# Last stage of a graph and expert kernel: more row and result buffers, groups computed ahead placed farther apart, the experts' bias added by TensorE

## What is computed

```python
x = x + segment_sum((layernorm(x) @ W)[src] * weight[:, None], dst) + b
xn = layernorm(x)                       # [12500, 256]
# routing is by the mean over all nodes, so that all nodes share two experts
top_w, top_i = top_k(routing(mean(xn) @ Wr + br), 2);  top_w = softmax(top_w)
y = sum_k top_w[k] * (gelu(xn @ W1[top_i[k]] + b1[top_i[k]]) @ W2[top_i[k]] + b2[top_i[k]])
x = x + layer_norm(y + xn) * gamma + beta
```

## Time and profile before

| | us |
|---|---|
| median of 3 runs | 2519.41 |
| lowest and highest | 2519.26, 2525.82 |
| the profiled execution | 2519.76 |
| its span in the profile | 2518.0 |
| PE busy over the span | 2178.6 |
| DVE, ACT, POOL busy | 1054.8, 1145.3, 1656.8 |
| last stage, first `up` to the last matmul | 2019.4 to 2505.4 |

### The profile page before, as it was taken

How to read it: one execution, slowest core, us unless ns; L and a number is a source line. 1 busy time by engine, 2 the same in 40 slices (tenths; PEclk the granted TensorE clock), 3 DMA queues, 4 the chain that set the end, 5 groups by cost and what they waited for, 6 DMA issues and landing times. The chain is left out here.

```text
span 2518.0 us, 40482 instructions
## 1 busy us (share of the span) xinstructions
PE 2178.6 (87%) x9536; PEld 1651.2 (66%) x9537; DVE 1054.8 (42%) x2962; ACT 1145.3 (45%) x3139; POOL 1656.8 (66%) x1643
## 2 busy tenths in 40 slices
PE   2388898889989988899989989889899889888898
PEld 1266666666767665676666666666676678777787
DVE  7693222232332232232232223223233257778876
ACT  3467666565564444443333233322311265544453
POOL 6577777777777777777777777777777413434332
PEclk9899999999999998999999999999999989999999
DMA  9955555555655555555555546555555422322221
GB/s 339 305 163 163 164 166 162 170 176 173 222 183 177 162 173 158 172 174 172 161 164 168 165 149 193 161 161 166 171 165 172 131 97 93 101 84 84 84 77 54
DMA packets 229382, 401.22 MB, mean 159 GB/s; under 512 B 35813, under 2 KB 150170, under 8 KB 229244
## 3 DMA queue, kind: packets, MB, share of 16 engines
q0 software_dynamic: 75072, 205.10, 27.5%
q1 hardware_dynamic: 153740, 192.37, 23.7%
q10 hardware_dynamic: 432, 2.40, 0.3%
HBM read 323.27 MB, written 76.46 MB: 159 GB/s over the span
## 5 line engine op out<-in xcount | busy, mean ns | idle before, releaser
L515 POOL DMA_INDIRECT G<-xr_d,SRC x1468 | 1390.9, 947 | 447.2 <-issue 297.3
L970 DVE TENSOR_SCALAR OH<-CST,DL,WR 128x128 f32<-128x128 f32 x1564 | 571.0, 371 | 1273.5 <-PE ps L1240 747.0
L1240 PE MATMUL ps<-G,OH 128*128 x3128 | 744.7, 390 | 141.6 <-DVE OH L970 130.1
L1240 PEld LDWEIGHTS ps<-G,OH 128*128 128x128 f32 x3128 | 597.3, 194 | 283.6 <-issue 204.6
L1219 PE MATMUL ps<-YU,W1u 128*128 128x512 f32 x768 | 358.6, 620 | 58.6 <-ACT H L697 31.1
L1230 PE MATMUL ps<-W2u,H 128*128 128x256 f32 x1536 | 347.4, 385 | 7.2 <-issue 6.9
L1230 PEld LDWEIGHTS ps<-W2u,H 128*128 128x128 f32 x1536 | 292.4, 192 | 58.6 <-issue 19.5
L1219 PEld LDWEIGHTS ps<-YU,W1u 128*128 128x128 f32 x768 | 147.7, 198 | 248.5 <-issue 207.3
L704 ACT ACTIVATE YE<-ps 128x512 f32<-128x512 f32 x96 | 57.3, 597 | 445.9 <-PE ps L1230 445.9
L697 ACT ACTIVATE H<-ps,b1a 128x512 f32<-128x512 f32 x192 | 130.9, 687 | 275.6 <-PE ps L1219 275.4
L1072 DVE TENSOR_TENSOR Hlo<-Ht,Hhi 128x512 fp32r<-128x512 f32 (+1 forms) x152 | 135.5, 898 | 115.7 <-ACT Hhi L796 115.6
(11 more groups left out here) (170 smaller groups left out, 2494.5 us busy)
## 6 DMA issues: line engine op xcount, KB each, us to landing
W1u<-in_W SPq DMA_DIRECT2D x48, 512.0 KB
W2u<-in_W SPq DMA_DIRECT2D x48, 512.0 KB
y_d<-YE SPq DMA_DIRECT2D x48, 512.0 KB
G<-xr_d,SRC POOLq DMA_INDIRECT x1468
x_d<-X SPq DMA_DIRECT2D x98, 128.0 KB, 2.5
yt_d<-YT SPq DMA_DIRECT2D x98, 128.0 KB, 2.4
XR<-in_x SPq DMA_DIRECT2D x97, 128.0 KB
XS<-in_x SPq DMA_DIRECT2D x24, 512.0 KB, 12.9
```

Source lines behind the costliest of these rows:

```text
L515: e.indirect_dma_start(out=G[:, s % RING, :], out_offset=None, in_=x if s < FRESH else xr_d, in_offset=bass.IndirectOffsetOnAxis(ap=SRC[:, ...
L970: e.tensor_scalar(OH[:, s % OHR, :], iota, DL[:, s:s + 1], WR[:, s + 1:s + 2], ALU.is_equal, ALU.mult).then_inc(s_oh, 1)
L1240: e.matmul(ps[:, 0, 0:D], OH[:, r, :], Gf[:, bass.ds(g + r * D, D)], start=False, stop=True, skip_group_check=True).then_inc(s_main, 1)
```

## The change

- `XL` gets a fourth buffer, and SP loads item n + 4 behind item n. `Z` and its statistics get a third buffer. `XN` keeps three. SP loads four `XL` at the start of the stage.
- The groups computed ahead stand behind `post[1]`, `[3]`, `[6]`, `[9]`, `[11]` and `[14]`.
- Of the 19 post groups POOL no longer adds the bias (L523 stays for the six groups computed ahead). DVE splits the bias once into a high and a low row, `B2r`, in four small instructions. In `down(k, 7)` each tile gets one more matmul, 2 partitions by 128x256, that adds both rows: 74 in all.
- POOL adds the rows of two items ahead before `rstd`, if the next item is a group computed ahead.
- `YP[0]` takes the room of `W2s`, so the first four `YP` loads wait until the low half of W2 is made. The load of `YL` for `post[2]` now goes ahead of them.
- In the first part some semaphores are merged (x, xr, router loads). Who waits for what stays.

```diff
-            if k >= 1 and k % 2 == 1 and len(pre_of) < AHEAD:
-                pre_of[k] = len(pre_of)
-                order.append(pre_of[k])
+        pre_of = {1 + (len(post) - 3) * a // AHEAD: a for a in range(AHEAD)}
+        order = [n for k, g in enumerate(post) for n in ((g, pre_of[k]) if k in pre_of else (g,))]
...
-            for n in range(3):
+            for n in range(4):
                 load_x1(n)
...
-            e.wait_ge(s_w1l, 2)
-            for a in range(2):
-                load_y(a)
...
             load_yl(2)
+            e.wait_ge(s_w1l, 2)
+            e.wait_ge(s_w2l, 2)
+            for a in range(2):
+                load_y(a)
...
-                if n + 3 < NG:
-                    load_x1(n + 3)
+                if n + 4 < NG:
+                    load_x1(n + 4)
...
-                e.wait_ge(s_b2, 2)
-                e.tensor_tensor(out=XN[:, n % 3, 0:m, :], in0=XN[:, n % 3, 0:m, :], in1=B2[:, :].unsqueeze(1).to_broadcast([P, m, D]), op=ALU.add).then_inc(s_xb, 1)
+                if g < AHEAD:
+                    e.wait_ge(s_b2, 2)
+                    e.tensor_tensor(out=XN[:, n % 3, 0:m, :], in0=XN[:, n % 3, 0:m, :], in1=B2[:, :].unsqueeze(1).to_broadcast([P, m, D]), op=ALU.add).then_inc(s_xb, 1)
...
-            add_rows(0)
+            added = 0
             for n in range(NG):
-                if n + 1 < NG:
-                    add_rows(n + 1)
+                until = min(n + (2 if n + 1 < NG and order[n + 1] < AHEAD else 1), NG - 1)
+                while added <= until:
+                    add_rows(added)
+                    added += 1
                 rstd(n)
...
+            e.wait_ge(s_b2, 2)
+            e.tensor_copy(B2h[:, :], B2[0:2, :]).then_inc(s_b2, 1)
+            e.wait_ge(s_b2, 3)
+            e.tensor_tensor(out=B2l[:, :], in0=B2[0:2, :], in1=B2h[:, :].bitcast(f32), op=ALU.subtract).then_inc(s_b2, 1)
+            e.wait_ge(s_b2, 4)
+            e.tensor_scalar(B2t[:, :], B2l[:, :].bitcast(f32), ident[0:2, 1:2], None, ALU.mult).then_inc(s_b2, 1)
+            e.wait_ge(s_b2, 5)
+            e.scalar_tensor_tensor(out=B2r[:, :], in0=B2h[:, :].bitcast(f32), scalar=ident[0:2, 0:1], in1=B2t[:, :], op0=ALU.mult, op1=ALU.add).then_inc(s_b2, 1)
...
-                        e.wait_ge(s_xb, n + 1)
-                        if n >= 2:
-                            e.wait_ge(out_st[n % 2], 16 * (n // 2))
+                        if g >= AHEAD:
+                            e.wait_ge(s_xn, n + 1)
+                        else:
+                            e.wait_ge(s_xb, g + 1)
+                        if n >= 3:
+                            e.wait_ge(out_st[n % 3], 16 * (n // 3))
...
-                        ins = e.matmul(acc, hp[:, h, rows], wp[:, x_, f, :], start=(i == 0 and q % 2 == 0 and a == 0), stop=(i == HID - 1 and a == 2), skip_group_check=True)
+                        ins = e.matmul(acc, hp[:, h, rows], wp[:, x_, f, :], start=(i == 0 and q % 2 == 0 and a == 0), stop=False, skip_group_check=True)
+                    if i == HID - 1:
+                        e.wait_ge(s_b2, 6)
+                        ins = e.matmul(acc, ones_r[:, :], B2r[:, :], start=False, stop=True, skip_group_check=True)
```

More of the change, by code:

```diff
@@ L128, in gnn_ffn @@
         base = (nc.sbuf_base + 31) // 32 * 32
-        ARENA = 48896
+        ARENA = 49152
         sb("arena", [P, ARENA])
@@ L195, in gnn_ffn @@
         late = At()
-        YL, XL = late("YL", [P, 2, 2, GT * P]), late("XL", [P, 3, GT, D])
+        YL, XL = late("YL", [P, 2, 2, GT * P]), late("XL", [P, 4, GT, D])
         YTh, YTl = late("YTh", [P, 2, 2, GT * P], f32r), late("YTl", [P, 2, 2, GT * P], f32r)
@@ L199, in gnn_ffn @@
         XN = late("XN", [P, 3, GT, D])
-        W2h, W2l, W2s = late("W2h", [P, 2, 4, D], f32r), late("W2l", [P, 2, 4, D], f32r), late("W2s", [P, 2, 4, D])
+        W2h, W2l = late("W2h", [P, 2, 4, D], f32r), late("W2l", [P, 2, 4, D], f32r)
+        w2s_at = late.at
+        W2s = late("W2s", [P, 2, 4, D])
+        B2h, B2l, B2t, B2r = late("B2h", [2, D], f32r), late("B2l", [2, D], f32r), late("B2t", [2, D]), late("B2r", [2, D], f32r)
         Ht = late("Ht", [P, HB, GT * P])
@@ L203, in gnn_ffn @@
         assert late.at - 4 * HID * GT * P <= 4 * ARENA - 4 * E * 2 * F
-        YP, Z = late("YP", [P, 2, 2, GT, D]), late("Z", [P, 2, GT, D])
+        YP = At(w2s_at)("YP0", [P, 2, GT, D]), late("YP1", [P, 2, GT, D])
+        Z = late("Z", [P, 3, GT, D])
         def row(v):
@@ L241, in gnn_ffn @@
         s_w1h, s_w1l, s_w2h, s_w2l, s_b2 = sem("act_w1h"), sem("dve_w1l"), sem("act_w2h"), sem("dve_w2l"), sem("dve_b2")
-        b2_in, xl_in = sem("b2_in"), [sem(f"xl_in{k}") for k in range(3)]
+        b2_in, xl_in = sem("b2_in"), [sem(f"xl_in{k}") for k in range(4)]
         yl_in, yp_in = [sem(f"yl_in{k}") for k in range(2)], [sem(f"yp_in{k}") for k in range(2)]
@@ L248, in gnn_ffn @@
         s_zr, s_zg, s_fin, s_b1s = sem("pool_zr"), sem("dve_zg"), sem("dve_fin"), sem("dve_b1")
-        out_st, out_last = [sem(f"out{k}") for k in range(2)], sem("out_last")
+        out_st, out_last = [sem(f"out{k}") for k in range(3)], sem("out_last")
         ends = range(0, FRESH + 1, 8)
@@ L444, in load_x1 @@
                 m = len(tiles(order[n]))
-                e.dma_start(XL[:, n % 3, 0:m, :], x1_d[order[n], :, 0:m, :]).then_inc(xl_in[n % 3], 16)
-            for n in range(3):
+                e.dma_start(XL[:, n % 4, 0:m, :], x1_d[order[n], :, 0:m, :]).then_inc(xl_in[n % 4], 16)
+            for n in range(4):
                 load_x1(n)
@@ L753, in normal2 @@
                 for j, t in enumerate(tiles(g)):
-                    ins = e.activation(XN[:, n % 3, slot(t), :], XL[:, n % 3, slot(t), :], ACT.Identity, bias=NR[:, t:t + 1], scale=R1[:, t:t + 1])
+                    ins = e.activation(XN[:, n % 3, slot(t), :], XL[:, n % 4, slot(t), :], ACT.Identity, bias=NR[:, t:t + 1], scale=R1[:, t:t + 1])
                 ins.then_inc(s_xn, 1)
@@ L1078, in total @@
                     if q == 0:
-                        e.wait_ge(s_xb, n + 1)
-                        if n >= 2:
-                            e.wait_ge(out_st[n % 2], 16 * (n // 2))
-                        if n >= 2 and order[n - 2] == 0:
+                        if g >= AHEAD:
[4 more added lines that the diff above has]
+                            e.wait_ge(out_st[n % 3], 16 * (n // 3))
+                        if n >= 3 and order[n - 3] == 0:
                             e.wait_ge(out_last, 16)
```

63 lines of the change are left out of this document (27 added, 36 removed).

## The result

The changed kernel takes 2500.51 us (median of 4 runs, 2497.67 to 2503.14) against 2520.65 of the kernel before (4 runs). The ratio is 0.9914, with a 95% interval of 0.9899 to 0.9928. So it is faster by 0.9%, where 2.0% was forecast: 30 us above the forecast and 8 above the range. The profiled execution took 2503.14 us, the longest of the four and 2.6 above their median; its span is 2501.3.

A forecast was written before the change was run, and what follows sets the result against it. PE was taken to bound the last stage, losing 57.4 us to stalls and low clock around groups computed ahead. Sum: 2519.76 - 57.4 + 8.8 (bias) - 1.0 (start) = 2470.2, forecast 2470 us, range 2461 to 2492.

The forecast's parts named there:

- The bias on PE: Last stage: 74 added bias matmuls at 0.119 us each, priced like same-width neighbours, cost 8.8 us on PE's path.
- the start: Start of the last stage: 1 us booked as gained, in a range from 6 gained to 2.5 lost.
- The upper end: Bias matmuls in the last stage: 74 at the 0.38 us duration of the lone L1199, 28 us.
- dear bias matmuls: Rival, last stage: bias matmuls don't run in the stream with the others, 28 us instead of 8.8, so 2489; chance 0.07.
- The loss of 57.4 us: 134 steps from up(1, 2) to up(18, 0): 39.8 us PE idleness plus 17.6 of lower clock, all taken as gained.
- The XL wait: ACT's wait for rows at groups computed ahead, 61.3 us in ten waits: four buffers and spreading remove it altogether.
- The step by which `YL` comes 7.4 us earlier: First group computed ahead: its last give ends at 2115.2 instead of 2122.6, against 6.0 us of PE idleness to cover.
- POOL and DVE: 19 of 25 POOL bias additions go, freeing at most 40 us of DVE; no time of its own booked.
- a cover: Fewer DVE meetings with POOL, at most 40 us of DVE, serve only to secure the earlier YL and YTl.
- The YL wait: Behind groups computed ahead: ACT still waits, six waits of 3 to 6 us, but PE doesn't, by 1.4 us margin.
- the collision: Start of the stage: POOL's L525 addition meets the second W1l, holding it 2 us or more; in full 2.5 lost, 2474.
- the forecast's low end: Lower bound of the forecast time for the whole kernel, given as 2463 in one place and 2461 in another.

The follow-up runs named there:

- e1: The change with the bias matmul over 128 partitions, zeros below the second row; last stage 447.5 us against 481.2 in the change, ratio to the kernel before 0.9875.
- e11: Kernel before with the fourth row buffer (and third result buffer, later YP loads, merged semaphores), bias on POOL, old places and order; last stage 471.5 us against 498.6.
- e7: e1 with three row buffers, row loads three items ahead, all else kept; last stage 450.3 us against 447.5.
- e10: e1 with three row buffers, old places of the groups computed ahead and POOL's old order, bias still on PE; last stage 468.5 us against 498.6 before.
- e2: The change with the wait for B2r only once, ahead of the first down, still 2 partitions; last stage 475.2 us against 481.2.
- e5: e1 with the bias matmul over 64 partitions instead of 128; last stage 475.3 us against 447.5.
- e3: The change with a group's four bias matmuls in a row behind its other matmuls, 2 partitions; last stage 454.5 us against 481.2.
- e8: e1 with POOL waiting ahead of its first addition until DVE has made the second YTl; last stage 444.4 us against 447.5.

## Why the prediction was wrong

**The bias on PE** is the step that failed. It booked 74 x 0.119 = 8.8 us, as if a matmul over 2 partitions ran in the stream like one over 128. Measured are 74 x 0.50 = 37.0, since each holds up its neighbours, and e1 shows that the row count does it. The profiled execution also lost 4.6 us at half clock behind three eighth steps. Put these into the prediction's own sum: 2470.2 + 28.2 + 4.6 = 2503.0, and the profiled execution took 2503.14. That it meets so closely is luck: the start gained 0.45 us of the 1 booked, the last stage began 0.7 later, and the end of the stage, with six of the matmuls, is 1.8 us longer and not 3. Against the median of 2500.51 the sum is 2.5 too high.

The upper end, 28 us, was wrong too, and that is what pushed the result out of the range. It took the duration of L1199 for its price. The duration leaves out what the neighbours lose. The trace of the kernel before had it, in rows that the prediction doesn't draw on:

```profile
1997.14 0.38 PE L1198 MATMUL ps<-Wsb,AT 128*128 128x256 f32 x1
1997.44 0.18 PEld L1199 LDWEIGHTS ps<-b2r,ones_r 2*128 2x128 f32 x1 [0.33 <-issue]
1997.45 0.38 PE L1199 MATMUL ps<-b2r,ones_r 2*128 2x256 f32 x1
1997.76 0.33 PE L1203 MATMUL ps<-CST,XH 128*128 128x128 f32 x1
```

It starts 0.31 us behind its predecessor and the next instruction 0.31 behind it, where the matmuls of L1198 start 0.22 apart; ahead of its weight load the loads stand still for 0.33 us with no releaser. The view of L1199 from which the earlier trace rows come has that idle time as 37.0 us in 106 times. The reading that failed is that it "stands alone there": it has a matmul close on either side. As a rival "dear bias matmuls" was named with a chance of 0.07 and 2489 us, on the ground that they don't run in the stream; that happened, and was a third dearer (37.0 against 28).

The load of weights over 2 partitions is no longer than others, 182 ns, against 190 for those over 128. But in the change it starts together with its matmul, at 2087.97, and so does the load of the matmul behind it, at 2088.28; the load of the one behind that starts 0.11 us ahead, as loads do between equal neighbours. By the rule of the Trainium skill that the prediction cites (TensorE: Matmul & The Clock Gate, section LDWEIGHTS) a load takes the same time whatever its partitions. The trace agrees, but the cost isn't in the duration of the load.

**The loss of 57.4 us** and that it goes: right. PE isn't idle from 2047 to 2480, and in e1 the stage is 51.1 us shorter than before, 57.4 - 8.8 + 1 being 49.6. With the 128 partitions the forecast of 2470 would have held, as far as the stage tells (2520.65 - 51.1 = 2469.6; e1 as a whole wasn't timed beside a kernel of 2520 us). The prediction read the earlier trace rows as full clock from 2414 on; the row has 0.98, the rest of the last half-clock stretch.

**The XL wait**: it went, as counted by the steps. That it was the root of all the stalls was wrong. The fourth buffer alone gives 27.1 us of the 57.4 (e11), and from e1 without it only 2.8 are lost (e7). The step by which `YL` comes 7.4 us earlier for the first group was worked out with the lighter POOL already in it; the text then gave all of it to the rows. In e11 the `YL` waits only fell from 67.2 to 57.2 us.

**POOL and DVE**: "no time of its own is booked" was the wrong book. Of the parts tried alone the additions off POOL are the largest, 38.9 us (e10, with the matmuls' 8.8 added back). The 40 us of DVE were worked out there and then called a cover. The total of 57.4 came out right although much of the gain was put down to the wrong part; so far that is luck.

**The YL wait**: right that it stays in ACT without reaching PE: in e1 five waits, 18.9 us in all, 3.8 each, where six of 3 to 6 us were forecast. How much margin there was, 1.4 us or another, no run measures. In the change itself they are smaller (4.9 us in four), which fits its longer steps.

**The start**: the collision came, but held the copy of b1s and not the second W1l. `YTl` came at 2039.44, as before at 2039.45, and from the first `up` to `up(1, 2)` it was 27.4 us instead of 27.8. 0.4 gained, 1 booked. (The forecast's low end stands in the prediction as 2463 and as 2461; nothing here hangs on it.)

**Spreading** is worth 1.3 us when all else is there. The third result buffer wasn't tried by itself.

## What to carry to other kernels

Keep the row count of neighbouring matmuls the same. A bias of two rows is cheaper with zeros down to 128 partitions, or at least with all such matmuls in one run. Price an instruction by the starts on both sides of it, in a place where it has the neighbours that it will have, and not by its duration. And where several parts each remove a stall, try each alone and take each out before crediting any: three parts here gain 12 to 39 us alone, and 1 to 4 us when they come last, and the costly matmuls hid the stalls too.

## What the runs showed of the hardware

- A matmul over 2 or 64 partitions among matmuls over 128 costs 0.50 us, 0.38 more than one over 128 (128x256; the change, e2, e5 against e1); four in a row cost 0.84 together (e3).
- The granted clock fell from 1.00 to 0.51 behind four such matmuls at three of 17 places in the change, while the trace shows PE busy all the time. In e2 and e5, with the same slow steps, it stayed at 1.00 at all 17, as it did with 128 partitions (e1) and with the four in a row (e3). The cause is open.
- A DVE copy of 4 elements a partition, with a single input, took 2.34 us beside a POOL addition of two SBUF tiles and 0.16 us without it (the change, e8).
